# Wo's bias added to the loaded residual by GpSimd, in place of four bias products a batch on TensorE

## The reference

```
xn  = layernorm(x)
q   = ln_head(xn @ Wq + bq)          # 16 heads of 32, normalised per head
k,v = ctx_main @ Wk + bk, ... Wv + bv;   k = ln_head(k)
kd,vd = ctx_dca @ Wkv_dca + bkv_dca;     kd = ln_head(kd)
a   = attn(q, k, v) + attn(q, kd, vd)
x2  = x + (a @ Wo + bo)              # bo is what this change is about
n2  = layernorm(x2)
out = x2 + down(silu(gate(n2)) * up(n2))     # weights looked up in a table of 16 values
```

## Time and profile before

| | us |
|---|---|
| median of 3 executions | 836.38 (835.38 to 836.42) |
| the profiled execution | 836.12 |
| its span in the trace | 834.3 |
| TensorE matmuls busy | 768.4 (92%) |
| VectorE busy | 521.3 (62%) |
| ScalarE busy | 489.4 (59%) |
| GpSimd busy | 232.6 (28%) |

### The profile page before, as it was taken

One profiled execution on the slowest core, in us unless ns is written; L12 is line 12 of the kernel. 1 busy time (PEld: TensorE's weight loads), 2 busy tenths in 40 slices (PEclk: granted clock), 3 DMA queues, 4 the chain that ended last, 5 costly groups with the idle time before them and its releaser, 6 DMA issues.

```text
span 834.3 us, 14792 instructions
## 1 busy us (share of the span) xinstructions
PE 768.4 (92%) x5842; PEld 314.9 (38%) x5842; DVE 521.3 (62%) x1007; ACT 489.4 (59%) x996; POOL 232.6 (28%) x248
## 2 busy tenths in 40 slices
PE   3776665999899999999999999999999999999998
PEld 1342221333354334223543343234543332355445
DVE  7879999898566996322849982318589911062211
ACT  3567878788265886664548875654578856511100
POOL 6782111000364222002551221005722210013320
PEclk9998878899999999999999999999999999999999
DMA  7738886486230000222300002222100000000001
GB/s 246 185 110 233 215 226 169 128 190 142 83 72 1 1 1 1 66 63 76 77 2 2 1 2 51 64 60 71 12 1 2 2 26 26 27 26 1 0 13 39
DMA packets 72532, 56.50 MB, mean 68 GB/s; under 512 B 33232, under 2 KB 60624, under 8 KB 72464
## 3 DMA queue, kind: packets, MB, share of 16 engines
q1 hardware_dynamic: 72128, 55.31, 25.1%
q10 hardware_dynamic: 208, 0.26, 0.1%
q0 software_dynamic: 128, 0.00, 0.0%
HBM read 40.67 MB, written 8.45 MB: 59 GB/s over the span
## 4 chain that ended last, share of the span: by engine, by line
PE 70%; DVE 20%; ACT 3%; issue 2%; POOL 1%; DMA 1%; SPq 1%; DVEq 0%; POOLq 0%; ACTq 0%
PE ps L1359 50%; PE ps L1633 7%; PE ps L1614 5%; DVE arena L903 5%; DVE nmax L1158 3%; DVE nmax L1159 3%; PE ps L1587 3%; DVE nmax L1155 3%; PE ps L1410 3%; ACT ps L800 2%; DVE arena L910 2%; PE ps L1533 2%; PE ps L1620 1%; DMA arena<-idx 1%; POOL hrstd L596 1%
## 5 line engine op out<-in xcount | busy, mean ns | idle before, releaser
L1359 PE MATMUL ps<-arena,wf_hi 128*128 128x512 f16 (+2 forms) x736 | 211.1, 371 | 4.0 <-DVE arena L910 3.0
L800 ACT ACTIVATE ps<-ps,nmax 128x496 f32<-128x496 f32 x256 | 165.8, 649 | 26.7 <-DVE nmax L1158 26.7
L828 ACT ACTIVATE arena<-ps 128x1024 f32<-128x1024 f32 x128 | 124.2, 1024 | 74.0 <-PE ps L1620 74.0
L1359 PE MATMUL ps<-arena,wf_lo 128*128 128x512 f16 (+2 forms) x368 | 136.1, 370 | 0.0
L1359 PE MATMUL ps<-wf_hi,arena 128*128 128x512 f16 (+3 forms) x374 | 114.8, 368 | 0.0
L596 POOL TENSOR_TENSOR hrstd<-hvar,mhalf 128x16 f32<-128x16 f32 (+1 forms) x33 | 98.1, 2986 | 47.0 <-DVE hvar L1007 46.7
L1359 PEld LDWEIGHTS ps<-arena,wf_hi 128*128 128x128 f16 (+1 forms) x736 | 69.4, 100 | 90.2 <-DVE arena L910 13.1
L1410 PE MATMUL ps<-arena,wf_lo 128*32 128x512 f16 (+1 forms) x1056 | 73.4, 425 | 21.4 <-ACT wf_lo L667 21.2
L903 DVE TENSOR_SCALAR arena<-arena,wf_lo 128x2048 f16<-128x2048 f16 (+1 forms) x132 | 89.2, 737 | 5.2 <-PE ps L1410 3.9
L572 POOL TENSOR_TENSOR xrstd<-xvar,mhalf 128x1 f32<-128x1 f32 x32 | 20.0, 626 | 213.4 <-DVE xvar L945 213.4
L1359 PE MATMUL ps<-wf_lo,arena 128*128 128x512 f16 (+3 forms) x187 | 68.5, 366 | 0.0
(11 more groups left out here) (137 smaller groups left out, 1060.7 us busy)
## 6 DMA issues: line engine op xcount, KB each, us to landing
arena<-idx SPq DMA_DIRECT2D x124, 128.0 KB, 3.2
arena<-in_x SPq DMA_DIRECT2D x32, 256.0 KB, 3.0
wf_lo<-in_idx SPq DMA_DIRECT2D x10, 512.0 KB, 4.9
idx<-wf_hi SPq DMA_DIRECT2D x10, 384.0 KB, 3.1
out<-arena SPq DMA_DIRECT2D x15, 256.0 KB, 2.0
wf_lo<-in_idx SPq DMA_DIRECT2D x11, 256.0 KB, 6.2
arena<-in_ctxT SPq DMA_DIRECT2D x4, 512.0 KB, 4.6
arena<-in_Wq SPq DMA_DIRECT2D x4, 256.0 KB, 4.9
```

The costliest lines, as they stand in the source:

```text
L800: last = act.activation(sc, sc, ACT.Exp, bias=nmax[:, 0, t, h:h + 1], accum_out=den[:, 0, t, h:h + 1])
L828: act.activation(probs[n_ % 2][:, 2 * p:2 * p + 2, :], ps[:, bank:bank + 2, :], ACT.Exp).then_inc(s["probs_set"], 1)
L1359: last = pe.matmul(dst, l, r, start=(first and i == 0), stop=(stop and i == len(todo) - 1))
```

## The change

bo is no longer a row block of `b16`. A new tile `out_bias` (128 x 512, float32) gets bo on every row by one DMA from ScalarE's queue. `add_bias(t, bt)` on GpSimd adds it to x2's tile t as soon as the residual has landed, and counts `res_set`; VectorE's `residual` waits for `res_set` in place of `res_in`. The thirteenth product of each tile goes on TensorE, at all 16 tiles. GpSimd's two memsets of `sel["o"]` go, and so does the second of the two `bias_low` instructions. Rows 64 to 127 of `st_b` are filled with bq, only so that they hold numbers.

```
+BIAS_AT = {4: 0, 10: 1, 15: 2}
...
-        sel = {n: sb("sel_" + n, [P, P], F16) for n in ("q", "k", "d", "o")}
+        sel = {n: sb("sel_" + n, [P, P], F16) for n in ("q", "k", "d")}
+        out_bias = sb("out_bias", [P, D], F32)
...
-            link(pool.memset(sel["o"][0:64, :], 0.0))
-            link(pool.memset(sel["o"][64:P, :], 1.0 / 32))
...
+            def add_bias(t, bt):
+                pool.wait_ge(s["bo_in"], 16)
+                pool.wait_ge(s[f"res_in{t}"], nth(bt, 16, 16))
+                pool.tensor_tensor(x2[:, t, :], x2[:, t, :], out_bias[:, :], ALU.add).then_inc(s["res_set"], 1)
...
+                    first = not sum(prev)
                     dca_keys(a)
                     rstd(0)
+                    add_bias(0 if first else T - 1, prev)
                     rstd(1)
-                    tail(prev)
+                    if first:
+                        add_bias(1, prev)
+                    norm(2, 0, prev)
+                    if first:
+                        add_bias(2, prev)
+                    norm(2, 1, prev)
+                    if first:
+                        add_bias(3, prev)
+                    norm(2, 2, prev)
+                    norm(2, 3, prev)
...
                 for n_ in range(G * T):
                     if nxt is not None and n_ in NORM_AT:
                         norm(1, NORM_AT[n_], nxt)
+                    if prev is not None and n_ in BIAS_AT:
+                        add_bias(BIAS_AT[n_], a)
...
-            tail((B - 1, 0))
+            add_bias(T - 1, (B - 1, 0))
+            for t in range(T):
+                norm(2, t, (B - 1, 0))
...
-            act.dma_start(st_b[64:P, :], row("bo", 0, D).to_broadcast([64, D])).then_inc(s["bias_in"], 16)
+            act.dma_start(st_b[64:P, :], row("bq", 0, D).to_broadcast([64, D])).then_inc(s["bias_in"], 16)
+            act.dma_start(out_bias[:, :], row("bo", 0, D).to_broadcast([P, D])).then_inc(s["bo_in"], 16)
...
             def residual(t, bt):
-                dve.wait_ge(s[f"res_in{t}"], nth(bt, 16, 16))
+                dve.wait_ge(s["res_set"], nth(bt, T, t + 1))
...
-                for lo in (32, 96):
-                    rows_ = slice(lo, lo + 32)
-                    low(b16[rows_, :], st_b[rows_, :], b16[rows_, :]).then_inc(s["b_lo"], 1)
+                low(b16[32:64, :], st_b[32:64, :], b16[32:64, :]).then_inc(s["b_lo"], 1)
...
                             [(both(lambda a_: aT[a_][g][:, t * P:(t + 1) * P]), both(lambda a_: wo[a_][:, g, :])) for g in range(G)]
-                            + [(sel["o"][:, :], b16[:, :])]).then_inc(s["wo_done"], 1)
+).then_inc(s["wo_done"], 1)
...
-                product(dst, [(sel["o"][:, :], b16[:, :])] + [head_rows(g) for g in range(G - 1)], True, False)
+                product(dst, [head_rows(g) for g in range(G - 1)], True, False)
```

More of the change, by code:

```diff
@@ L317, in xattn_ffn @@
             sq_eps oh_set oh_used l_out
-            x_in0 x_in1 x_in2 x_in3 ctx_in res_in0 res_in1 res_in2 res_in3 out_stored0 out_stored1 out_stored2 out_stored3
+            x_in0 x_in1 x_in2 x_in3 ctx_in res_in0 res_in1 res_in2 res_in3 bo_in res_set out_stored0 out_stored1 out_stored2 out_stored3
             cT_hi cT_lo cd_in cd_hi cd_lo kd_set vd_in
@@ L582, in dca_keys @@
                     pool.tensor_copy(kT[i][:, :, 0:DCA], kd[i][:, :, cols]).then_inc(s["kd_set"], 1)
-            def tail(b):
-                for t in range(T):
-                    norm(2, t, b)
+            def add_bias(t, bt):
+                pool.wait_ge(s["bo_in"], 16)
+                pool.wait_ge(s[f"res_in{t}"], nth(bt, 16, 16))
+                pool.tensor_tensor(x2[:, t, :], x2[:, t, :], out_bias[:, :], ALU.add).then_inc(s["res_set"], 1)
             def core(a, before, between, nxt, prev):
@@ L1483, in project @@
                         if prev is None and u == 0:
-                            pe.wait_ge(s["b_lo"], 2)
+                            pe.wait_ge(s["b_lo"], 1)
                             pe.wait_ge(s["sel_set"], 1)
```

## The result

The changed kernel takes 840.34 us (median of 10 executions, 838.55 to 842.63), the kernel before 836.44 us (10 executions, 835.38 to 837.68). The ratio is 1.0049 [1.0037, 1.0061]: slower by 0.49%, 3.9 us. The forecast was 837.3 with a range up to 840.3, so the median lies just above the range.

What follows compares the result with a forecast made beforehand. TensorE, busy 92% of the span and 70% of the chain, was taken as the bound, with VectorE cushions of about a microsecond deciding; -0.7 + 1.25 + 0.60 - 0.27 = +0.9 us gave 837.3 us, range 833.4 to 840.3.

Steps and rivals of the forecast that it cites:

- the turnover of core 1: Turnover of core 1: four additions between the powers make VectorE late and TensorE wait; +1.25 us.
- `norm(2, 0)` (0.56) to 228.09, `standardise(0)` right behind it: Core 1's turnover: standardise follows the norm at once, with residual(1) 0.46 later, from 228.55 to 229.23.
- one more collision: Rival, core 1: additions of tiles 2 and 3 get in before standardise, L950 waits 1.16 us twice; 839.6; chance 0.16.
- The additions' length: Sixteen additions on GpSimd, taken as 1.16 us each from the row of its subtraction.
- Products, 3.46 us: TensorE: 16 bias products removed at 0.22 us, 0.86 at each turnover and the last tail; saving all spent.
- Cores 2 and 3: Their turnovers: the addition holds context_lo, rstd(1) comes late and TensorE waits; +0.30 us each, +0.60 together.
- gap 0.80 before the fourth group: Sign in cores 2 and 3: TensorE gap of 0.8 us ahead of its fourth wo group, released by L991.
- Power first: Rival, turnovers: GpSimd's next power reads before the held context_lo is let in; sum -2.0, 834.4 us; chance 0.22.
- Everything hidden: Rival: additions take 0.8, don't meet VectorE, all products and head count; -4.2, 832.2; 0.15 shared with another case.
- The last tail: Last tail: late addition nearly absorbed by VectorE's waiting, only the last of four bias products counts; -0.27 us.
- The head: Head: one bias_low goes from VectorE, on the chain for 0.69 us; -0.7 us, bounds 0 and -2.0.
- the clock in the head: Rival, head: TensorE's clock drop is spared, 1.3 us less; with the forecast 836.0; no separate chance given.

Runs made afterwards that it cites:

- e11: The changed kernel run again, unchanged, beside other kernels on one chip; 840.33 us, ratio to before 1.0061.
- e12: e3 run again, beside e11 on one chip; 837.52 us, ratio to before 1.0026.
- e5: e4 without its three GpSimd waits for the standardise; 836.25 us, ratio to before 1.0007.
- e8: Unchanged copy of e4, run again as neighbour of other kernels on one chip; 833.02 us, ratio to before 0.997.
- e3: The changed kernel, but in core 1 GpSimd's additions of tiles 2 and 3 wait until VectorE's standardise of the tile before is done; 838.81 us, ratio to before 1.0043.
- e4: The changed kernel with its sixteen additions moved: core 1 tiles 0, 1 before the first power, the turnovers' and tail's others behind norm and standardise; 833.29 us, ratio 0.9968.
- e1: The changed kernel without GpSimd's sixteen additions, bo left out of the result; 831.91 us, ratio to before 0.9958.
- e2: The changed kernel, additions kept, with a thirteenth product put back on TensorE at each tile; 840.84 us, ratio to before 1.0062.
- e9: e4 with twelve further idle subtractions on VectorE in the head, TensorE waiting for all; 839.80 us, ratio to before 1.0059.
- e6: e4's order in cores 2 and 3 and the last tail, the changed kernel's order in core 1; 837.19 us, ratio to before 1.002.
- e10: Unchanged copy of e4, run a third time as neighbour of other kernels on one chip; 832.66 us, ratio to before 0.9968.
- e7: e4 with five further idle subtractions on VectorE in the head, TensorE waiting for all; 834.54 us, ratio to before 0.9989.

## Why the prediction was wrong, step by step

**What failed is the turnover of core 1**, forecast +1.25, measured +3.41 (and +3.42 in e11). The step that said "`norm(2, 0)` (0.56) to 228.09, `standardise(0)` right behind it" let VectorE in first. It was the rival *one more collision*, given 0.16, that happened: the addition queued behind the norm starts 0.06 us before VectorE, twice. Counted from the core's start, `residual(1)` begins at 15.61 where I had 14.50, and `normalise(2)` 4.5 us later than before where I had 2.43: two meetings of 0.93 and 0.18 from the additions' length. The rival's price was nearly right too, 839.6 for a measured 840.3, though it held VectorE 1.16 us a time: a meeting costs 0.93. Part of that nearness is luck: the price was 0.5 us too high for the two meetings and left out the 0.7 us at the end. e12 against e11, and e5 against e8, show the meetings' price by removing and by adding them alone. With the two meetings removed (e3, e12) the turnover is 31.36, +1.55 where the forecast had +1.25, so the rest of this term was nearly right. Of the 4.27 us between the change and e4 in core 1, 2.4 come from the first two additions, which stand between the powers, and 1.9 from the meetings.

**The additions' length**, taken as 1.16, was 1.26 to 1.27: the row of the subtraction was near, not equal. It adds 0.1 us at each addition on the path, some 0.2 in core 1.

**Products, 3.46 us.** Their price was right (0.86 a turnover in e1 against before), and so was the claim that it is all spent (e2).

**Cores 2 and 3**, forecast +0.30 each: +0.40 without disturbance (30.21 in e2, e3, e11). The mechanism held in every link: power behind the held `context_lo` (3.96 at core 2), gap 0.80 before the fourth group, foretold as 0.8. *Power first* falls: in core 1 `context_lo`, already waiting, was let in at 222.87, and the power behind the addition took 3.89. *Everything hidden* falls for this order; that its figure of 832.2 is nearly what the placed order gives is a coincidence in part, since it had the additions at 0.8 us and meeting nobody.

**The last tail**, forecast -0.27: -0.18, and +0.03 in e11, where in both the addition ended late against the first norm's due time.

**The head**, forecast -0.7: the group of wv starts at 27.23 in place of 27.94 and the scores at 58.11 in place of 58.88, and e9 shows that such a difference reaches the end. The rival *the clock in the head* turned out to be a matter of the execution, not of the change (last section).

**What the sum left out** is the 0.7 us behind the last transposition and outside the span. The prediction took the 1.8 us outside the span as unchanged without a reason and looked at nothing behind the tail.

**Together** the terms are -0.77 + 3.41 + 0.40 + 0.40 - 0.18 = +3.3, and +4.0 with the 0.7, for +3.9 [3.1, 5.1] measured. For e4 against before they are -0.77 - 3 x 0.86 - 0.87 = -4.2, and -3.5 with the 0.7, for -2.5 to -2.7 measured by the three ratios, whose intervals reach to -3.6 or beyond. So nothing more is shown to be missing; up to 1 us may be, and the scatter of core 1's start hides it in single profiles. Two candidates are late transposes, which cost 0.7 to 1.3 us in four of the thirteen later profiles and none in before's one, and the 256 KB load of `out_bias` in the head; neither was tried alone. The profiled execution of the change is 2.3 us above the median, of which 1.3 are the late transpose in its core 3.

So the positions alone (4.27 us in core 1, 1.26 in each of two cores, 0.7 to 0.9 in the tail) decide between 840 and 833 us. The version to keep is e4.

## What to carry to other kernels

When an instruction goes on GpSimd beside a VectorE stream that is waited for, its own length (1.27 us here) is not the price. Look which VectorE instruction is released by the GpSimd instruction just ahead of it: where it was an addition that had nothing else to wait for, the two started within 0.1 us of each other each time here, the GpSimd one first, and the VectorE one took 0.93 us longer. The mend is either a wait for the other engine's instruction (e3, e4: 0.93 us back a time) or a place where nobody waits for what is held: the meetings of the attention phases lost the same 0.93 us at no cost. And price the change at the first round apart from the steady ones: core 1, with four additions in place of one, held 3.4 of the 4.0 us that the turnovers and the tail lost.

## What the runs showed of the hardware

**Who blocks whom, and for how long.** Addition of 1.26 us on GpSimd against a VectorE instruction with only SBUF operands: the latter is held until 0.13 us (`context_lo`, 1.67 for 1.22) or 0.26 us (standardise, 1.48 for 0.55) before the addition's reported end. Held the other way, a power of 16 columns grew from 2.91 to 3.89 and one of a single column from 0.55 to 0.93; the latter was as long in the kernel before (0.94 at 228.01), beside a VectorE conversion with two SBUF inputs. A standardise has one full-size input and two columns of scalars, and is held like `context_lo` with its two. But a power in progress doesn't hold `context_lo` (1.22 inside 5.79 in e4). The Trainium skill says that a VectorE instruction with two SBUF inputs and a GpSimd one that reads SBUF contend for an exclusive lock, and that whoever is first holds such a lock for the whole instruction (SBUF — State Buffer, "Who interferes with whom"). In these traces that is nearly so for the addition (all but its last 0.13 to 0.26 us), and not so for the power.

**The clock after a wait in the head.** e4 and e6 are the same program up to core 1. In both, TensorE waited 3.28 us for the same instruction and took up work again within 0.01 us of the other. In e4 its granted clock was then 0.53 in the window from 28 to 30 us, nearly its level of 1.2 GHz, and in e6 1.00, 2.4 GHz. TensorE's next group in e4 and that window:

```profile
27.21 4.06 PE L1377 MATMUL ps<-wv,arena 128*128 128x512 f16 x12 [3.28 <-DVE arena L1000]
...
28.00:30.00 2.00, 2.00 (x6) 0.76 (x5) 2.00 (x5) 0.00 (x0) 1.65 (x1) 0.53 0.00 0
```

and in e6:

```profile
27.22 2.75 PE L1380 MATMUL ps<-wv,arena 128*128 128x512 f16 x12 [3.28 <-DVE arena L1003]
...
28.00:30.00 2.00, 2.00 (x11) 0.88 (x9) 2.00 (x5) 0.00 (x0) 1.65 (x1) 1.00 0.00 0
```

The scores then begin at 58.15 or at 56.41. The profile of the changed kernel shows 0.50 and its second one, e11, shows 1.00. Four profiled executions (e2, e6, e10, e11) had the full clock there, two of them (e10 and e11) after a shorter wait, of 2.19 and 2.27 us. So this one event gives or takes 1.7 us (1.1 us more in e3 and e5, where the low level lasted longer) from execution to execution, part of the 4 us over which those of one kernel spread. In e7 TensorE had other work until 29.98, and the group of wv came at 30.81 and took 2.75: of 3.6 us of delay 1.7 were paid back, 1.6 of it by this group's clock.
